# Quantising behind even units, the bias on Pool, and other places for blocks and reductions

## What is computed

```python
q = _split_heads(query @ q_w.T + q_b, 16) / sqrt(16)      # 16 heads of 16 columns
k = _split_heads(query @ k_w.T + k_b, 16)
v = _split_heads(query @ v_w.T + v_b, 16)
attn = softmax(einsum('bhqd,bhkd->bhqk', q, k))           # 4096 x 4096 per head
out = merged_heads(attn @ v) @ out_w.T + out_b
# ffn: input and weight rounded to fp8 (e4m3) with one scale each
acc = x_fp8 @ w_fp8.T
ffn = (acc * (x_scale * w_scale) + bias).astype(bfloat16)
x = x + out + ffn
```

## Time and profile before

| | |
|---|---|
| median of 3 runs | 1831.96 us (1831.79 to 1832.84) |
| the profiled execution | 1832.19 us, its span 1830.3 us |
| ScalarE busy | 1734.1 us, 95% |
| TensorE matmul busy | 1631.1 us, 89% |
| VectorE busy | 1622.4 us, 89% |
| Pool busy | 48.2 us, 3% |
| granted TensorE clock, mean | 0.999 |

### The profile page before, as it was taken

One profiled execution on the slowest core, in us unless ns is written; L12 is line 12 of the kernel. 1 busy time (PEld: TensorE's weight loads), 2 busy tenths in 40 slices (PEclk: granted clock), 3 DMA queues, 4 the chain that ended last, 5 costly groups with the idle time before them and its releaser, 6 DMA issues.

```text
span 1830.3 us, 74852 instructions
## 1 busy us (share of the span) xinstructions
PE 1631.1 (89%) x33478; PEld 558.8 (31%) x33478; DVE 1622.4 (89%) x1876; ACT 1734.1 (95%) x1898; POOL 48.2 (3%) x71
## 2 busy tenths in 40 slices
PE   7998999899899889899888889898898989899887
PEld 4532222222222222222222222222222222222224
DVE  8889989899898989989888998989899898989988
ACT  2499999999999999999999999999999999999993
POOL 0000000000000000000000000000000000000000
PEclk9999999999999999999999999999999999999999
DMA  7401111110111111011110101101000100100113
GB/s 206 143 17 39 36 39 39 32 34 14 42 36 34 44 31 26 23 42 36 34 32 16 35 19 30 25 17 33 21 21 15 25 19 16 27 15 15 31 26 113
DMA packets 127081, 68.59 MB, mean 37 GB/s; under 512 B 77792, under 2 KB 117664, under 8 KB 126752
## 3 DMA queue, kind: packets, MB, share of 16 engines
q1 hardware_dynamic: 126272, 63.54, 13.3%
q10 hardware_dynamic: 480, 0.20, 0.0%
HBM read 41.93 MB, written 17.27 MB: 32 GB/s over the span
## 4 chain that ended last, share of the span: by engine, by line
ACT 45%; issue 26%; PE 18%; DVE 9%; DMA 0%; ACTq 0%; SPq 0%; DVEq 0%
ACT probs L916 45%; PE banks L1666 8%; PE banks L1610 4%; DVE bits L1272 2%; PE banks L1632 2%; PE banks L1521 1%; PE banks L1511 1%; DVE horner L1279 1%; DVE horner L1285 1%; DVE powers L1282 1%; DVE d_probs L1290 1%; PE banks L1793 1%; DVE powers L1276 1%; PE banks L1682 0%; ACTq L915 0%
## 5 line engine op out<-in xcount | busy, mean ns | idle before, releaser
L916 ACT ACTIVATE probs<-banks 128x1024 f32<-128x1024 f32 x1856 | 1711.1, 1116 | 12.4 <-PE banks L1610 5.2
L1666 PE MATMUL banks<-probs,v_st 64*32 64x512 f32 x14848 | 971.1, 590 | 0.3 <-DVEq L1254 0.2
L1610 PE MATMUL banks<-q_st,k_st 50*32 50x512 f16 x16384 | 764.7, 381 | 172.5 <-ACT probs L916 158.0
L1610 PEld LDWEIGHTS banks<-q_st,k_st 50*32 50x32 f16 x16384 | 229.9, 89 | 1070.9 <-ACT probs L916 907.5
L1272 DVE TENSOR_SCALAR bits<-banks 128x1024 int32<-128x1024 f32 x192 | 235.0, 1224 | 64.3 <-PE banks L1610 57.6
L1666 PEld LDWEIGHTS banks<-probs,v_st 64*32 64x32 f32 x14848 | 266.2, 106 | 58.4 <-issue 1.4
L1282 DVE SCALAR_TENSOR_TENSOR powers<-powers,horner 128x1024 f32<-128x1024 int32 x192 | 235.7, 1228 | 6.6
L1279 DVE SCALAR_TENSOR_TENSOR horner<-powers 128x1024 f32<-128x1024 int32 x192 | 235.4, 1226 | 6.6
L1285 DVE SCALAR_TENSOR_TENSOR horner<-powers,horner 128x1024 f32<-128x1024 f32 x192 | 235.2, 1225 | 6.6
L1290 DVE SCALAR_TENSOR_TENSOR d_probs<-horner,bits 128x1024 int32<-128x1024 f32 x192 | 235.2, 1225 | 6.6
L1276 DVE TENSOR_SCALAR powers<-bits 128x1024 int32<-128x1024 int32 x192 | 133.3, 694 | 6.6
(11 more groups left out here) (117 smaller groups left out, 460.4 us busy)
## 6 DMA issues: line engine op xcount, KB each, us to landing
late_x<-xnT_copy SPq DMA_DIRECT2D x32, 256.0 KB, 3.3
k_st<-k_parts SPq DMA_DIRECT2D x96, 64.0 KB, 2.3
q_st<-q_parts SPq DMA_DIRECT2D x186, 32.0 KB, 1.9
k_st<-k_parts SPq DMA_DIRECT2D x96, 60.0 KB, 2.2
xnT_copy<-probs SPq DMA_DIRECT2D x8, 512.0 KB, 3.4
q_st<-neg_row SPq DMA_DIRECT2D x256, 1.0 KB, 1.7
w_f<-xnT_copy SPq DMA_DIRECT2D x16, 256.0 KB, 2.9
xn_all<-ctx_out SPq DMA_DIRECT2D x128, 32.0 KB, 2.2
```

Of the source, the lines that this page charges most:

```text
L916: act.activation(probs[:, at:at + WIDE * CHUNK].rearrange("p (t c) -> p t c", t=WIDE), banks[:, bank:bank + WIDE, :], ACT.Exp, bias=EXP_SHIFT,
L1610: last = pe.matmul(banks[cols, bank + g, :], k_st[rows, keys], blocks[rows, j], start=True, stop=True, tile_position=(g * GROUP, t * VCOLS))
L1666: last = pe.matmul(banks[VCOLS * qb:VCOLS * (qb + 1), 6 + half, :], v_st[keys, kt, :], src[keys, g * CHUNK:(g + 1) * CHUNK], start=at == 0 ...
```

## The change

- Quantising part i moves from behind odd units to behind units 2, 3, 4, 6, 8, ... 30 (QUANTISE_BEHIND), the weight's part from unit 0 to unit 1; SyncE's loads move along (load_quantised).
- The output bias is added to x_all by Pool, in 16 additions of two tiles behind the all-reduce of the maxima; VectorE's first early_part waits for them.
- Units 18 to 30 use the late units' places for D blocks and maximum (even: maximum at 21 instead of 22; odd: second D block at 13 instead of 12); unit 31 has D blocks at 7, 16, 25 instead of 9, 18, 27 and its first early output at 34 instead of 33.
- The four reciprocals stand apart between D blocks and places of units 16 and 30; scale_context runs two at a time behind odd units, and the first ones of each half behind a first D block.
- Prologue: the reductions of |xn| are eight over four tiles each, behind values of m = 3 (three, and that of w_f), 5 (four) and 6 (one); V of the last chunk is projected in pieces at places 2, 3 and 4 of unit 0; ScalarE waits for the saves of xnT in two halves, ahead of exponentials 0 and 4; SyncE issues load_rows and the last save_turned earlier.
- The ffn of the last four tiles stands ahead of output 2 instead of 1.

```diff
--- before.py
+++ after.py
@@ -100,12 +100,10 @@
     LATE_COLS = CHUNK // 2
-    EARLY_D_AT = ((4, 13, 25, 37, 45, 55), (4, 12, 25, 36, 45, 54))
-    EARLY_MAX_AT = (22, 21)
-    EARLY_AT = (33, 63)
+    EARLY_AT = LATE_AT
...
     EARLY = (HEADS * UNITS - FIRST_EARLY) * len(EARLY_AT)
-    LAST_D_AT = (9, 18, 27, 37, 46, 55)
+    LAST_D_AT, LAST_EARLY_AT = (7, 16, 25, 37, 46, 55), (34, 63)
@@ -153,7 +151,7 @@
         ln = sb("ln", [P, 6, 8])
-        amax = sb("amax", [P, 2, 8])
+        amax = sb("amax", [P, 2, NCH + 1])
@@ -232,11 +230,12 @@
         xn_ready = sem("xn_ready")
+        amax_part = sem("amax_part")
...
         xT_ready = sem("xT_ready")
-        xT_saved = sem("xT_saved")
+        xT_saved = [sem(f"xT_saved{i}") for i in range(2)]
@@ -262,6 +261,7 @@
         y_done = sem("y_done")
+        biased = sem("biased")
@@ -274,7 +274,10 @@
         FLAG_AT = 5
-        FFN_AT = 1
+        FFN_AT = 2
+        QUANTISE_BEHIND = (2, 3, *range(4, HEADS * UNITS, UNITS))
+        RECIPROCALS_AFTER = {(LATE_UNITS, D_AT[0]): (0, 0), (LATE_UNITS, MAX_AT): (0, 1),
+                             (HEADS * UNITS - 2, LATE_MAX_AT): (1, 0), (HEADS * UNITS - 2, EARLY_AT[0]): (1, 1)}
@@ -366,8 +369,8 @@
                     [Layout(D_AT, MAX_AT) for u in range(UNITS)],
-                    [Layout(EARLY_D_AT[u], EARLY_MAX_AT[u], EARLY_AT) for u in range(UNITS)],
-                    [None, Layout(LAST_D_AT, None, EARLY_AT)]]
+                    [Layout(LATE_D_AT[u], LATE_MAX_AT, EARLY_AT) for u in range(UNITS)],
+                    [None, Layout(LAST_D_AT, None, LAST_EARLY_AT)]]
@@ -420,6 +423,8 @@
         FIRST_Q, FIRST_MAX = 5, 6
+        LARGEST_AT = ((), (), (), (0, 1, 2), (), (3, 4, 5, 6), (7,), ())
+        LAST_V_AT = {2: (0, 1), 3: (2,), 4: (3,)}
@@ -450,7 +455,7 @@
             if h == HEADS - 1:
-                return range(8 + 2 * u, 10 + 6 * u)
+                return range(SCALES // KD + 2 * u, SCALES // KD + 2 + 6 * u)
@@ -584,7 +589,7 @@
                 sp.wait_ge(xT_ready, m * 2 + 2)
-                sp.dma_start(xnT_dram[:, :, span(CHUNK_AT[m] * CHUNK, CHUNK)], xnT[m]).then_inc(xT_saved, 16)
+                sp.dma_start(xnT_dram[:, :, span(CHUNK_AT[m] * CHUNK, CHUNK)], xnT[m]).then_inc(xT_saved[m // (NCH // 2)], 16)
@@ -638,7 +643,11 @@
             for m in range(NCH):
-                save_turned(m)
+                if m < NCH - 1:
+                    save_turned(m)
+                if m == FIRST_MAX:
+                    load_rows(first, 0, 1)
+                    save_turned(NCH - 1)
@@ -646,14 +655,13 @@
                     load_k(first, 0, 0)
-                if m == FIRST_MAX - 1:
-                    load_rows(first, 0, 1)
...
             load_q(sp, first, 0, 1)
-            sp.wait_ge(xT_saved, 16 * NCH)
+            for i in range(2):
+                sp.wait_ge(xT_saved[i], 16 * NCH // 2)
@@ -677,6 +685,13 @@
                                          buf[:, a, :].rearrange("r (j x) -> r j x", j=QB)).then_inc(saved, 16)
+            def load_quantised(n):
+                if n in QUANTISE_BEHIND:
+                    i = QUANTISE_BEHIND.index(n)
+                    sp.wait_ge(xq_used, i + 1)
+                    sp.dma_start(xq, xnT_dram.rearrange("p k s -> p (k s)")[:, i * CHUNK:(i + 1) * CHUNK]).then_inc(xq_in, 16)
@@ -707,6 +722,7 @@
                         load_rows(c, 1, h * 2 + 2)
+                        load_quantised(h * UNITS)
@@ -717,10 +733,6 @@
                         load_q(sp, c, nxt, 0)
-                    if not c.full:
-                        sp.wait_ge(xq_used, h + 1)
-                        half_cols = xnT_dram.rearrange("p k s -> p (k s)")
-                        sp.dma_start(xq, half_cols[:, bass.ds(h * CHUNK, CHUNK)]).then_inc(xq_in, 16)
@@ -728,6 +740,7 @@
                             load_rows(c, 0, h * 2 + 3)
+                        load_quantised(h * UNITS + 1)
@@ -806,7 +819,14 @@
             pool.wait_ge(amax_ready, 1)
-            pool.partition_all_reduce(amax_all[:, :], amax[:, :, 7], P, RMAX).then_inc(amax_shared, 1)
+            pool.partition_all_reduce(amax_all[:, :], amax[:, :, NCH], P, RMAX).then_inc(amax_shared, 1)
+            pool.wait_ge(of_bias_in, 16 * 4)
+            pool.wait_ge(xn_first, 1)
+            pool.wait_ge(xn_ready, NCH // 2)
+            for t in range(0, NT, 2):
+                pool.tensor_tensor(x_all[:, t:t + 2, :], x_all[:, t:t + 2, :], bo_sb[:, :, :], ALU.add
+                                   ).then_inc(biased, 1)
@@ -818,7 +838,7 @@
                 lay, i = first.layout(h, u), (h * UNITS + u - FIRST_EARLY) * len(EARLY_AT) + slot
-                pool.wait_ge(first.d_taken, first.take_0(h, u) + lay.takes.index(EARLY_AT[slot]) + 1)
+                pool.wait_ge(first.d_taken, first.take_0(h, u) + lay.takes.index(lay.late_at[slot]) + 1)
@@ -900,7 +920,6 @@
                         act.activation(late_w[:, i], w_sb[name][:, :, P:2 * P], ACT.Copy).then_inc(late_w_ready, 1)
-            act.wait_ge(xT_saved, 16 * NCH)
@@ -912,6 +931,8 @@
+                    if not c.full and h == 0 and a % (NCH // 2) == 0 and a < NCH:
+                        act.wait_ge(xT_saved[a // (NCH // 2)], 16 * NCH // 2)
@@ -1103,16 +1124,18 @@
-            def largest_of_x(g):
-                link(dve.tensor_reduce(amax[:, 0, g:g + 1], xn_all[:, g * 8:(g + 1) * 8, :], AX.XY, ALU.max,
-                                       apply_absolute_value=True))
+            def largest_of_x(m):
+                first_tile = CHUNK_AT[m] * CT
+                dve.tensor_reduce(amax[:, 0, m:m + 1], xn_all[:, first_tile:first_tile + CT, :], AX.XY, ALU.max,
+                                  apply_absolute_value=True).then_inc(amax_part, 1)
+                if m == 0:
+                    dve.wait_ge(w_in["f"], 16)
+                    dve.tensor_reduce(amax[:, 1, NCH:NCH + 1], wf_flat, AX.X, ALU.max, apply_absolute_value=True)
...
             def largest():
-                dve.wait_ge(w_in["f"], 16)
-                dve.tensor_reduce(amax[:, 0, 7:8], amax[:, 0, 0:4], AX.X, ALU.max)
-                dve.tensor_reduce(amax[:, 1, 7:8], wf_flat, AX.X, ALU.max, apply_absolute_value=True
-                                  ).then_inc(amax_ready, 1)
+                dve.wait_ge(amax_part, NCH)
+                dve.tensor_reduce(amax[:, 0, NCH:NCH + 1], amax[:, 0, 0:NCH], AX.X, ALU.max).then_inc(amax_ready, 1)
@@ -1143,7 +1166,7 @@
-            QUANT_STEPS = 5
+            QUANT_STEPS = 4
@@ -1221,9 +1244,11 @@
                     lay, i = c.layout(h, u), (h * UNITS + u - FIRST_EARLY) * len(EARLY_AT) + slot
-                    at = EARLY_AT[slot]
+                    at = lay.late_at[slot]
...
                     dve.wait_ge(c.st_done, c.place_0(h, u) + at + 1)
+                    if i == 0:
+                        dve.wait_ge(biased, NT // 2)
@@ -1310,15 +1335,13 @@
                         remainders(m)
-                        if m == NCH - 1:
-                            largest_of_x(3)
                         values(m)
-                        if NCH - 4 <= m < NCH - 1:
-                            largest_of_x(m - (NCH - 4))
-                    assert links[0] == LN_LINKS * LN_GROUPS + NCH // 2
+                        for position in LARGEST_AT[m]:
+                            largest_of_x(position)
+                    assert links[0] == LN_LINKS * LN_GROUPS
...
-                def quantise_part(h):
+                def quantise_part(h, n):
@@ -1327,7 +1350,7 @@
                     dve.wait_ge(xq_in, h * 16 + 16)
-                    dve.wait_ge(c.d_ready, block_at(h + 1, 0, 0))
+                    dve.wait_ge(c.d_ready, (n + 1) * D_BLOCKS)
@@ -1337,8 +1360,6 @@
                              fscale[:, 0, 2:3], qstep).then_inc(xq_used, 1)
-                    two = x_all[:, span(h * 2, 2), :]
-                    qstep(dve.tensor_tensor(two, two, bo_sb[:, :, :], ALU.add))
@@ -1350,25 +1371,23 @@
                             early_part(h, u, lay.late_at.index(p))
-                            if n == HEADS * UNITS - 2 and p == EARLY_AT[0]:
-                                reciprocals(1, 0)
-                                reciprocals(1, 1)
...
                             d_block(h, u, lay.d_at.index(p))
-                            if n == HEADS * UNITS - 1 and p != lay.d_at[0]:
+                            if n == HEADS * UNITS - 1:
                                 scale_context(SCALES // KD + lay.d_at.index(p))
-                    if n == HEADS * UNITS - 2:
-                        scale_context(SCALES // KD)
-                    if n == FIRST_SCALED - 1:
-                        reciprocals(0, 0)
-                        reciprocals(0, 1)
-                    if 0 <= n - FIRST_SCALED < SCALES // KD:
-                        scale_context(n - FIRST_SCALED)
+                            if n == FIRST_SCALED and p == lay.d_at[0]:
+                                scale_context(0)
+                        if (n, p) in RECIPROCALS_AFTER:
```

(35 more changed lines are left out.)

## The result

| | before | after |
|---|---|---|
| median | 1832.4 us (1831.79 to 1833.54, 4 runs) | 1844.4 us (1843.82 to 1845.16, 4 runs) |
| ratio, 95% interval | | 1.0065 (1.005 to 1.0081) |
| span of the profiled execution | 1830.3 us | 1843.1 us |

The change makes the kernel 12 us slower. The direction is the one forecast, the size is three times the forecast 3.95, and the time lies outside the range. The exponential's line, L916 before, is L937 now.

A forecast was written before the change was run, and what follows sets the result against it. The prediction took ScalarE's exponentials, busy 1711 us of a span of 1830, as the bound. Its terms, +1.5 + 0.4 + 8.5 + 2 - 0.2 - 4 - 1.65 - 2.6, gave +3.95 and 1835.9 us; range 1822 to 1840 (8 in 10).

The forecast's parts named there:

- Step 5: Units 1 to 17: -0.2 us, unit 1 shorter by 0.55, a D block in unit 16 late by 0.4.
- Step 2: First places of unit 0: +0.4 us, V tiles between the scores make three places late.
- step 3: Unit 0: +8.5 us, Pool's sixteen bias additions take turns with VectorE's instructions at 0.87 each.
- step 4: Unit 0: +2 us, TensorE's clock falls again behind two waits of over 3 us.
- Step 1: Prologue: first exponential +1.5 us later, the maxima in VectorE's queue delaying TensorE despite the removed wait of 3.46.
- Step 6: Units 18 to 30: -4 us from new places for maximum and D blocks.
- Step 7: Unit 31: -1.65 us from moved D blocks and early output, 55.45 becoming 53.8.
- Step 8: Tail: -2.6 us, VectorE takes the last sums without quantising and bias first, and the late FFN group moves.
- Pool yields: Rival, chance 0.24: in unit 0 Pool's additions slip in beside VectorE's, total -6.55 us, 1825.4.
- half the contention: Rival, chance 0.12: some additions fall where VectorE idles in unit 0, port cost 4, clock cost 1, run 1830.4 us.
- the prologue does not wait: Rival, chance 0.12: prologue's TensorE chain stays, first exponential at 78.7, -3.4 us instead of +1.5, run 1831.0.
- both: Rival, chance 0.05: Pool yields in unit 0 and the prologue does not wait for VectorE, run 1820.5 us.

The follow-up runs named there:

- e1: The changed kernel with unit 16's two reciprocals behind the D blocks at places 29 and 37: 1840.13 us (1.0043).
- e4: The changed kernel with bias on VectorE, maxima two by two behind chunks 4 to 7, unit 16's reciprocals behind its last D block: 1823.37 us (0.9957).
- e3: The changed kernel with the output bias added by VectorE again and Pool's 16 additions left out: 1833.7 us (1.0008).
- e7: The changed kernel with the old layout of unit 31 (D blocks at 9, 18, 27, early output at 33): 1848.67 us (1.0089).
- e2: The changed kernel with the maxima of x taken two by two behind chunks 4 to 7 of the prologue: 1840.92 us (1.0047).
- e14: e4 with the single wait for all eight saves and SyncE's old order both put back: 1825.71 us (0.9966).
- e6: The changed kernel with the old layouts of units 18 to 30 (D places and maxima): 1845.87 us (1.0077).

## Why the forecast was right in direction and short in size

**Step 5, units 1 to 17, is the step that failed: -0.2 forecast, +4.96 measured, 5.6 of it lost in unit 16.** The step priced the two reciprocals at their own duration, one D block late by 0.4. It didn't ask when their input lands. The load of the denominators is behind unit 15's saves in SyncE's queue in both kernels; the one before had it hidden, because its reciprocals stood at the unit's end. e1 gives 4.6 of the 5.6 back, e4 all of it. Of the 8.8 us that the whole sum fell short, 5.2 are this step; without unit 16's loss the median would have been near 1838.8, inside the range. Unit 1's -0.55 was right.

**Steps 2 to 4, unit 0: 10.9 forecast, 12.2 measured.** The mechanism was right: turns, the same five of a block's six instructions, and a fallen clock behind the two large waits. The turn was mis-sized: 0.87 from the earlier trace rows, 0.95 measured (2.18 less 1.23), and 0.9 for the first of the five (L1301, 1.60 instead of 0.70) where 0.5 was taken. The addition that the prediction took as 1.15 long lasted 1.27. Step 2 was right: three holes of 0.54, 0.38 and 0.59 where one of 1.05 stood. The additions began at 104.9, not 97, since 6.9 us that the profile puts down to issue lie between the all-reduce and the first addition. So no hole opened behind the transpose; the large ones stand behind the late item of place 33 and the D block of place 45. e3 puts clock and turns together at 11.4, against 10.5 in steps 3 and 4. No run takes the two apart, but VectorE alone was busy 10.5 longer with the additions in a row than in e3 (58.71 and 48.17).
The Trainium skill ("SBUF — State Buffer", section "SBUF: two separate sides") has the port pair as a lock held for a whole instruction, and the prediction set its own reading of one row above that rule. The trace of the changed kernel agrees with the rule for the small instruction: 1.28 us for 16 columns is a whole addition's wait. Within a D block it agrees only in part: the two-operand instructions start 2.22 us apart, less than 1.23 and 1.27 together, and a turn costs 0.95. By the estimate of 11 for step 3, steps 3 and 4 would have been 13; by the row they were 10.5, and 11.4 was measured.

**Step 1, the first exponential: +1.5 forecast, +3.13 measured.** Its chain came true in order: TensorE 3.0 late at chunk 5 (3.1 forecast), a second wait at the transpose. The idle 3.1 us, counted at 0 with an upper bound of 1.7, cost that bound: the projection behind the idle time took 5.4 instead of 3.6 at half clock. e3, with the same idle time and the clock at 1.00, shows that this can go either way, and e7 with 6.67 that it can cost more than the bound. e2, e4 and e14 size both halves: the new waits and order bring the first exponential from 82.4 to 78.3, the maxima take it to between 83.0 and 86.9, by how slow that projection turns out.
The Trainium skill ("TensorE: Matmul & The Clock Gate", section "Loop structure matters more than you think") has long waits between matmuls turn TensorE cold; the changed kernel and five of the runs agree, e3 shows that the same wait need not.

**Steps 6, 7 and 8** came out at -3.69, -1.70 and -2.12 against -4, -1.65 and -2.6. e6 shows the layouts as the cause of 2.9 us in the first, e7 of all of the second. In the tail the last unit's sums are taken at once, as forecast:

```profile
1818.69 0.69 DVE L1268 COPY o_sb<-banks 128x512 f32<-128x512 f32 x1 [1.79 <-PE banks L1690]
```

The tail's parts weren't tried one by one. Of the rivals, *Pool yields* falls with the 2.18 us, *half the contention* with e3's 11.4, *the prologue does not wait* with TensorE's two waits, and *both* with either.
